# Attention rounds in a layernorm, attention and mixture-of-experts kernel: a head's values ahead of a block of row maxima, two heads loaded on ACT's queue, stacked queries first on POOL

## The reference

```
x = x + layernorm(attention(layernorm(x)))
x = x + layernorm(moe(layernorm(x)))
```

```
ctx = local_attention(q, k, v)               # 8 blocks of 128 queries, 256 keys each
idx = [0, top 62 tokens by |q|, 1023]        # per head
ctx[idx] = softmax(q[idx] k^T / sqrt(32)) v  # 64 queries by 1024 keys
```

## Time and profile before

| | us |
|---|---|
| median of 3 runs | 916.54 (915.12, 916.54, 922.81) |
| profiled execution | 917.62 |
| its span | 915.9 |
| PE busy | 830.7 (91%) |
| DVE, ACT, POOL busy | 574.4, 401.6, 139.1 |
| mean granted TensorE clock | 0.951 of full |

### The profile page before, as it was taken

How to read it: one execution, slowest core, us unless ns; L and a number is a source line. 1 busy time by engine, 2 the same in 40 slices (tenths; PEclk the granted TensorE clock), 3 DMA queues, 4 the chain that set the end, 5 groups by cost and what they waited for, 6 DMA issues and landing times.

```text
span 915.9 us, 13743 instructions
## 1 busy us (share of the span) xinstructions
PE 830.7 (91%) x5060; PEld 680.6 (74%) x5060; DVE 574.4 (63%) x1230; ACT 401.6 (44%) x771; POOL 139.1 (15%) x199
## 2 busy tenths in 40 slices
PE   2999998979989999898969989989999999999994
PEld 2676766656767877676758778789999999887873
DVE  5545995447955465656348764436667777748565
ACT  2424232314445555454554334346666666623120
POOL 4000002120031001111112662100000000012232
PEclk9999999987989999899979899989999999999996
DMA  6696544874558566754025872256777777645443
GB/s 205 186 302 205 188 144 148 246 227 113 142 145 226 165 192 166 191 160 113 19 71 167 293 253 96 72 182 207 222 225 220 217 222 226 201 149 177 145 140 125
DMA packets 117442, 162.38 MB, mean 177 GB/s; under 512 B 17316, under 2 KB 65188, under 8 KB 117376
## 3 DMA queue, kind: packets, MB, share of 16 engines
q1 hardware_dynamic: 113792, 153.54, 55.2%
q0 software_dynamic: 3584, 7.97, 3.0%
HBM read 107.24 MB, written 55.05 MB: 177 GB/s over the span
## 4 chain that ended last, share of the span: by engine, by line
PE 76%; DVE 12%; ACT 4%; DMA 3%; issue 2%; POOL 1%; SPq 1%; DVEq 0%; POOLq 0%; ACTq 0%
PE bank L163 48%; PE wide L163 22%; PE wide L167 4%; PE bank L167 3%; DVE SG L160 2%; ACT PG L157 1%; DMA H<-scr_oe,FG 1%; DVE STC L273 1%; DVE XT L149 1%; DMA QSe<-MR 1%; DVE CX L1357 1%; DMA scr_xd<-H,FSI 1%; DMA scr_v<-vt 1%; DVE SIL L149 1%; DVE CX L154 1%
## 5 line engine op out<-in xcount | busy, mean ns | idle before, releaser
L163 PE MATMUL bank<-XT,W13H 128*128 128x256 f32 (+1 forms) x1056 | 244.2, 326 | 3.1 <-DVE XT L149 3.1
L163 PEld LDWEIGHTS bank<-XT,W13H 128*128 128x128 f32 x1056 | 177.0, 192 | 19.2 <-ACT W13H L145 1.9
L163 PE MATMUL bank<-XT,W13L 128*128 128x256 f32 (+1 forms) x528 | 170.5, 323 | 0.0
L163 PE MATMUL wide<-W2H,HH 128*128 128x512 f32 x352 | 120.5, 409 | 3.8 <-DVE CX L1357 3.6
L160 DVE TENSOR_REDUCE MX<-wide 128x1 f32<-128x192 f32 (+1 forms) x128 | 77.8, 649 | 71.0 <-PE wide L163 71.0
L163 PEld LDWEIGHTS bank<-XT,W13L 128*128 128x128 f32 x528 | 101.3, 192 | 8.3
L157 ACT ACTIVATE PT<-bank 128x512 f32<-128x512 f32 x128 | 72.5, 594 | 31.2 <-PE bank L163 31.0
L163 PEld LDWEIGHTS wide<-W2H,HH 128*128 128x128 f32 x352 | 69.8, 198 | 20.7 <-DVE CX L1357 5.3
L149 DVE TENSOR_TENSOR SIL<-bank,SIL 128x256 f32<-128x256 f32 (+1 forms) x72 | 36.8, 511 | 73.8 <-ACT SIL L157 73.2
L157 ACT ACTIVATE SIL<-bank 128x256 f32<-128x256 f32 (+1 forms) x72 | 32.7, 454 | 109.8 <-PE bank L163 108.7
L163 PE MATMUL wide<-W2L,HH 128*128 128x512 f32 x192 | 77.9, 406 | 0.0
(11 more groups left out here) (201 smaller groups left out, 1534.1 us busy)
## 6 DMA issues: line engine op xcount, KB each, us to landing
R<-in_L_ffn_W_dram SPq DMA_DIRECT2D x48, 512.0 KB, 5.3
scr_q<-hl SPq DMA_DIRECT2D x16, 512.0 KB, 4.3
scr_k<-hl SPq DMA_DIRECT2D x16, 512.0 KB, 3.8
R<-in_L_ffn_sw_dram SPq DMA_DIRECT2D x12, 512.0 KB, 4.3
QSe<-scr_q SPq DMA_DIRECT2D x36, 128.0 KB, 3.0
KSe<-scr_k SPq DMA_DIRECT2D x36, 128.0 KB, 3.3
scr_v<-vt SPq DMA_DIRECT2D x16, 272.0 KB, 2.1
R<-_attn_hidden_states_dram SPq DMA_DIRECT2D x16, 256.0 KB, 3.9
```

The source lines that it names most:

```text
L163: return do("pe", lambda g: g.matmul(ps, a, b, start=start, stop=stop, skip_group_check=True), after, mark=mark)
```

## The change

Four edits.

1. In slot 4 of each round the row maxima (block (1, 0) of head 2i + 3) are no longer ahead of `row_shift` and `local_values`; they come behind them.
2. Heads 2 and 3 are loaded by 12 DMAs on ACT's queue, not SP's, and wait for the last k product (`m_keys`), not for the last instruction that PE had been given.
3. `stack_q`'s POOL copies wait for `fence_ps`, not for the whole fence.
4. The memset of GT's middle third comes behind the first stack's copies on POOL.

```diff
-        def load_head(n, after=()):
+        def load_head(n, after=(), e="sp"):
...
-                mq = dma("sp", QS.slots[qi], lambda g, part=part, l=l: g.dma_start(
+                mq = dma(e, QS.slots[qi], lambda g, part=part, l=l: g.dma_start(
...
-                mk = dma("sp", KS.slots[ki], lambda g, part=part, l=l: g.dma_start(
+                mk = dma(e, KS.slots[ki], lambda g, part=part, l=l: g.dma_start(
...
+                m_keys = m_p
                 for j in range(4):
...
-                        first_maxima(j)
+                        first_maxima(j, m_keys)
...
-                    m_last = Q_last(Q, "pe")
...
-                            r.busy.append([m_last])
+                            r.busy.append([m_keys])
...
-                                         [m_last, Q_last(Q, "pool")]))
-                    load_head(2, kv_b0)
-                    load_head(3, kv_b0)
+                                         [m_keys, Q_last(Q, "pool")]))
+                    load_head(2, kv_b0, "act")
+                    load_head(3, kv_b0, "act")
...
-            m_zgt = do("pool", lambda g: g.memset(f(GT[:, :, 64:128]), 0.0), fence + [Q_last(Q, "pool")])
-
...
-                a1 = copy("pool", GS[:, :, 32:64], G[:, r, :], gm[8 * b + 4:8 * b + 8] + begun + gs_busy)
+                a1 = copy("pool", GS[:, :, 32:64], G[:, r, :], gm[8 * b + 4:8 * b + 8] + fence_ps + gs_busy + [Q_last(Q, "pool")])
...
+                if b == 0:
+                    m_zgt.append(do("pool", lambda g: g.memset(f(GT[:, :, 64:128]), 0.0), begun + [a3]))
...
-                                 [hd["mk"], m_gt[i // 8], m_zgt] + wfree, mark=(c == 1))
+                                 [hd["mk"], m_gt[i // 8]] + m_zgt + wfree, mark=(c == 1))
...
-                    if k in ROW_MAX and i < 15:
+                    if k in ROW_MAX and k != 4 and i < 15:
                         row_max(2 * i + 2 + ROW_MAX[k][0], ROW_MAX[k][1])
...
                 if g >= 4 and g % 4 == 0:
                     for u in range(4):
                         local_values(g // 4 - 1, u)
+                if k == 4 and i < 15:
+                    row_max(2 * i + 2 + ROW_MAX[k][0], ROW_MAX[k][1])
```

More of the change, by code:

```diff
@@ L605, in proj_group, with first_maxima @@
                             fence_ps.extend([m_p, m_v, Q_last(Q, "act")])
-                        first_maxima(j)
+                        first_maxima(j, m_keys)
                 HT.busy[hti].append(m_p)
-            def first_maxima(j):
+            def first_maxima(j, m_keys):
                 if j == 0:
-                    m_last = Q_last(Q, "pe")
                     W_.busy[:] = [qtp.busy[0] + m_nrm[-1:], tp.busy[0] + tp.busy[1]]
@@ L785, in stack_q @@
                 W_.busy[wi].append(m_gt[b])
-            gs_busy = []
+            gs_busy, m_zgt = [], []
             ct, ctx_stored, gp = {}, {}, {}
```

## The result

The changed kernel takes 927.99 us (median of 11 runs) where the kernel before takes 918.89 (11 runs): ratio 1.0101, 95% interval 1.0074 to 1.0127. Forecast were 927.5 and +11.0 us; measured are +9.1 and +12.0.

A forecast was written before the change was run, and what follows sets the result against it. PE, busy 830.7 of 915.9 us, was taken to bound the kernel through its list order and waits. Terms -3.7 + 6.5 + 8.2 = +11.0 on the profiled 917.6 gave 928.6, less 1.1 for the median: 927.5; range 917 to 933.

The forecast's parts named there:

- Edit 1, the order: Slot 4: the transpose waits for DVE, so moved maxima cost 0.5 us in each of 13 rounds, +6.5 us.
- Edit 1, the clock: Attention rounds: PE's longer waits let its clock fall more often, 1.64 us a fall, +8.2 us, ends 0 and 11.5.
- The count of five: Of seven rounds (2, 4, 6, 7, 8, 9, 12) that could newly have a clock fall, five were taken.
- Rival A: Attention rounds: the clock does not fall more often; 919.3 us, chance 0.24.
- Edit 2: Start: with loads on ACT's queue, head 0's row leaves SP 3 us earlier and head 1's chain moves by -3.7 us.
- the v addition is free when the last product ends: Start: the fourth v's addition can begin at 193.84 and end at 194.6 where it ended at 198.36.
- Rival C: Start: the loads on ACT cost what they save, so nothing is won there; 931.2 us, chance 0.08.
- Edits 3 and 4: Start, POOL: PE's wait of 1.84 us for GS goes, worth nothing by itself since head 1's row ends later.
- Rival B: Start, 199 to 216 us: the clock holds, about 4 us won beside the 3.7, kernel not slower; 915.3 us, chance 0.10.
- the chain that the prediction named: Start: 8.9 us from the fence to head 1's scores, all SP and DMA, including 12 loads ahead of head 1's row.

The follow-up runs named there:

- e3: Changed kernel with slot 4's transpose of MX moved behind the values and the block of maxima; 903.33 us against 914.31 for the kernel before.
- e1: Kernel before with only the third block of row maxima moved behind the values in slot 4; 930.31 us against 914.31.
- e10: The changed kernel measured again with fresh runs of the kernel before; 926.02 us against 914.02, ratio 1.0148.
- e8: Changed kernel plus four unused matmuls in slot 4 of rounds 1 to 14, ahead of the transpose of MX; 914.1 us against 914.21 for the kernel before.
- e2: Changed kernel with the row maxima put back in their old place, the other three edits kept; 910.59 us against 914.31 for the kernel before.
- e5: e3 with the loads of heads 4 and 5 behind head 1's row of shifts on SP's queue; 894.51 us against 914.21 for the kernel before.
- e9: e5 with the loads of heads 2 and 3 back on SP's queue; 902.04 us against 914.02 for the kernel before.
- e4: Kernel before with only the two POOL edits (stacked queries' copies behind the bank fence, memset behind them); 914.01 us against 914.31.

## Why the prediction was right, point by point

**Edit 1, the order.** Right, in mechanism and size. The transpose waits for DVE, the values wait behind it, and the moved block costs its own time: 0.46 us a round for 0.5. e3, which moves the transpose alone, shows that it was the gate.

**Edit 1, the clock.** Right in kind: e1 leaves 10.0 us for it, by estimate, where the sum had 8.2 with ends of 0 and 11.5. The count of five was a choice, and it varies: e10 has five new falls, and the first profile three, with one gone and 3.0 us in round 3, for which the prediction had no term. That its 8.2 met 5.3 us there and about 10 in e1 is in part luck. Rival A is refuted by e1, +16.0 where A had 6 to 7, and by e8: the same critical steps, more work, 11.9 us less. One figure beside the sum was wrong: four falls, not five, are enough to pass 925.7 (919.3 + 6.6 = 925.9). By the Trainium skill ("TensorE: Matmul & The Clock Gate", Part 1) the clock goes down after a stretch in which the engine is idle throughout. The trace does not agree that it takes one: the clock fell behind idle spells of 1.60 and 1.59 us (rounds 2 and 8) with matmuls close on both sides.

**Edit 2.** The time was right (-3.7 forecast, -3.7 in e2 by the medians, with an interval of about -4.6 to -0.9), the working of it was not, and the match is luck. The step that failed is "the v addition is free when the last product ends": the first v store needs until 194 to land beside ACT's loads (median landing 4.8 us for 2.9), the third vt waits 3.20 us for it, and so does the third store. Head 0's row stands behind that store in SP's list, and it left SP at 195.13 and not at 191.8. Head 1's scores gained 2.2 to 2.3 us in place of 3.7. The clock may have made up for the rest: it was low for less of the start (0.64 for 0.50 over 199 to 216 us). Rival C was right that the loads hold up the v stores from ACT's queue too, and wrong in size: the median landing is 4.5 to 4.8 us in the profiles with all 12 loads on ACT (changed kernel, e2, e3, e5), 2.9 and 3.1 with them on SP (before, e9). On ACT they also leave ahead of the first v store (186.44 for 188.02), and on SP behind it (187.24 for 186.88), so whether it is the load on the engines or the order stays open. ACT's issue itself is as dear as SP's, 1.29 to 1.84 us for three.

**Edits 3 and 4.** Right: 0 by e4, with PE's wait for GS turned into a longer one for head 1's row.

**Rival B** did not happen in the change, because of the chain that the prediction named, fence, 12 loads, row. e5 took the loads out of that chain, and then it did: clock at 1.00 over the whole 17 us.

## What to carry to other kernels

Before moving work ahead into a wait, look at what stands first in the new order and what releases *that*: a wait named after one engine can hide a second one that ends at nearly the same time. Work that ran inside the gap was free, and moving it out makes the gap longer and the full time fuller. When waits of TensorE are near the length behind which the clock has been seen to fall, price them with the fall, 1.64 us here, and not with their own length alone: filling a wait, even with useless matmuls, won back the cost of the whole change.

## What the runs showed of the hardware

Behind an idle spell of 1.57 to 1.60 us TensorE's clock fell in rounds 2 and 8 of the changed kernel and not in rounds 4, 5, 6, 7 and 9, with the same kind of work on either side; in e10, the same program, it fell in rounds 2, 5, 6, 8 and 9. Single executions of one program so differ in the number of falls, and the 11 runs of the changed kernel spread over 8.5 us (923.07 to 931.58). Moving three small things (a transpose, a row's DMA, 12 loads' queue) won 19.7 us here (894.51 for 914.21), at a mean granted clock of 0.975 over the runs of e5 for 0.957 of the kernel before beside them.
